# A transformer layer with experts on one core: the last tile's first norm, the routing plan and the end of the program

## The reference

```
x = x + xattn(layernorm(x), ctx, ctx)              # 16 heads, softmax, full context
x = x + linear_attn(layernorm(x))                  # elu features, cumulative k*v, its own layernorm
h = layernorm(x)
shared = (silu(h @ wg.T) * (h @ wu.T)) @ wd.T
topw, topi = top_k(sigmoid(h @ gate.T), 8);  topw /= topw.sum()
routed = sum over the 8: topw * ((silu(h @ eg[e].T) * (h @ eu[e].T)) @ ed[e].T)
x = x + shared + routed
```

## Time and profile before

| | us |
|---|---|
| median of 3 executions | 1316.6 (1314.49 to 1318.66) |
| the profiled execution | 1314.09 |
| its span, first to last instruction | 1312.2 |
| PE busy | 1231.6 (94%) |
| DVE busy | 743.8 (57%) |
| ACT busy | 593.5 (45%) |
| POOL busy | 395.9 (30%) |
| mean granted clock of PE, share of full | 0.986 |

### The profile page before, as it was taken

How to read it: one execution, slowest core, us unless ns; L and a number is a source line. 1 busy time by engine, 2 the same in 40 slices (tenths; PEclk the granted TensorE clock), 3 DMA queues, 4 the chain that set the end, 5 groups by cost and what they waited for, 6 DMA issues and landing times. The chain is left out here.

```text
span 1312.2 us, 32009 instructions
## 1 busy us (share of the span) xinstructions
PE 1231.6 (94%) x9830; PEld 926.3 (71%) x9831; DVE 743.8 (57%) x1645; ACT 593.5 (45%) x1184; POOL 395.9 (30%) x312
## 2 busy tenths in 40 slices
PE   5999999999999999999997789999999999999991
PEld 5888787877787878777875347766776676667660
DVE  4454765656657556565556656656555556556440
ACT  2443443433433434343341165667556666556540
POOL 0001021030020200300203224557554656556531
PEclk9999999999999999999999989999999999999996
DMA  6631200111102102101031177999999999999875
GB/s 224 279 125 35 68 20 17 68 35 35 52 18 68 34 3 68 36 26 52 2 106 33 57 251 246 314 317 344 301 302 285 310 330 335 337 270 323 260 189 88
DMA packets 67370, 205.44 MB, mean 157 GB/s; under 512 B 16064, under 2 KB 18496, under 8 KB 56913
## 3 DMA queue, kind: packets, MB, share of 16 engines
q1 hardware_dynamic: 43392, 159.78, 33.7%
q0 software_dynamic: 23888, 44.40, 16.2%
HBM read 177.32 MB, written 37.03 MB: 163 GB/s over the span
## 5 line engine op out<-in xcount | busy, mean ns | idle before, releaser
L452 POOL TENSOR_TENSOR rstd<-vep,half 128x1 f32<-128x1 f32 x32 | 20.7, 647 | 604.3 <-DVE vep L618 604.3
L917 PE MATMUL bank<-ch,wkh 128*128 128x256 f32 x512 | 157.1, 307 | 9.9 <-DVE cl L633 6.4
L543 ACT ACTIVATE kt<-bank,colb 128x256 f32<-128x256 f32 x128 | 60.5, 473 | 222.4 <-PE bank L919 222.4
L1621 PE MATMUL ebank<-guh,xth 128*128 128x512 f32 x380 | 155.5, 409 | 1.3 <-DVE xtl L1482 0.8
L1477 DVE TENSOR_TENSOR gul<-wgu,guh 128x2048 fp32r<-128x2048 f32 x54 | 123.8, 2292 | 53.7 <-ACT guh L1393 44.3
L1322 POOL DMA_INDIRECT xg<-xn_rows,ig x95 | 124.5, 1311 | 92.2 <-issue 60.6
L1623 PE MATMUL ebank<-guh,xtl 128*128 128x512 f32 x380 | 149.7, 394 | 0.0
L1622 PE MATMUL ebank<-gul,xth 128*128 128x512 f32 x380 | 148.9, 392 | 0.0
L918 PE MATMUL bank<-cl,wkh 128*128 128x256 f32 x512 | 144.9, 283 | 0.0
L919 PE MATMUL bank<-ch,wkl 128*128 128x256 f32 x512 | 144.9, 283 | 0.0
L1651 PE MATMUL ebank<-wd,ht 128*128 128x512 f32 x292 | 134.3, 593 | 0.8 <-ACT ht L1378 0.8
(11 more groups left out here) (242 smaller groups left out, 2475.4 us busy)
## 6 DMA issues: line engine op xcount, KB each, us to landing
wgu<-in_egu SPq DMA_DIRECT2D x54, 1024.0 KB
wd<-in_edn SPq DMA_DIRECT2D x54, 512.0 KB
sgu<-in_egu SPq DMA_DIRECT2D x17, 1024.0 KB
craw<-in_ctx SPq DMA_DIRECT2D x32, 514.0 KB, 3.3
sdn<-in_edn SPq DMA_DIRECT2D x17, 512.0 KB
wqkv<-in_wqkv SPq DMA_DIRECT2D x1, 3072.0 KB, 18.6
second_sums<-x1b SPq DMA_DIRECT2D x9, 256.0 KB, 4.0
xa<-in_x SPq DMA_DIRECT2D x8, 256.0 KB, 2.9
```

The lines of the kernel that those rows point to most:

```text
L917: mm(out, wkh[:, c, w], h[:, c, :], start=c == 0, stop=False)
L1621: mm(out, ah[:, c, :], bh[:, c, :], start=c == 0, stop=False)
```

## The change

Four edits:

1. The plan moves from the start of the second part into the first, as the function `plan()`, which DVE runs behind the shared addition of tile 2 (`PLAN` = 2) and so in front of that of tile 3. In the second part PE's four small products stand first.
2. Tile 7's first norm takes its statistics (`moments`) straight behind the addition; the waits for the store of `xn` and for `x3T` stand behind them, in front of the operation that writes `xn` (`normed`).
3. On POOL tile 7's residual moves ahead of tile 6's `outproj` roots, behind the last maximum of the attention (`s_nb`); its `xr` is loaded at tile 6's step `v`. Tile 7's `x1b` waits until `xn` has been written.
4. The second block is made with `no_gpsimd_drain=True`.

The split of the shared tiles, four and four, is the same in both kernels.

The diff. Of the plan's own lines, which are the same in both places, the first and the last stand:

```diff
@@ -79,6 +79,7 @@
 
 
 BIAS = 2
+PLAN = 2
 EARLY = K
 WRITE = 8
 
@@ -387,7 +388,7 @@
                     sp.dma_start(d.acc[bass.ds(t * P, P), :], x2[:, :]).then_inc(s_ys, 16)
                     if type(t) is int and t == NT - 2:
                         load_shared(t, d.sx[t - SHA], d.sy[t - SHA], d.s_sl)
-                if n == "outproj":
+                if n == ("v" if type(t) is int and t == NT - 2 else "outproj"):
 
                     xe_wait(sp, "oproj", t, tick)
                     if type(t) is not int or t + 1 < NT:
@@ -476,11 +477,15 @@
 
                     root(norm_pre(t))
 
+            def residual(t):
+                wait(pool, s_xr, 16 * (t + 1), tick)
+                nc.gpsimd.tensor_tensor(xr[:, :], xr[:, :], rowb[:, 0, :], ALU.add).then_inc(s_xb, 1)
+
             def on_post(n, t):
                 if n == "oproj":
                     wait(pool, s_wrest, 16 * 7)
-                    wait(pool, s_xr, 16 * (t + 1), tick)
-                    nc.gpsimd.tensor_tensor(xr[:, :], xr[:, :], rowb[:, 0, :], ALU.add).then_inc(s_xb, 1)
+                    if not (type(t) is int and t == NT - 1):
+                        residual(t)
                     root(norm_post(t, 0))
                     xe_wait(pool, "oproj", t, tick)
                     pool.wait_ge(s_blank, 16 * (NT + 1))
@@ -492,7 +497,12 @@
                                                          compute_op=ALU.add).then_inc(dumped, 16)
                         for dumped in d.s_dumped:
                             pool.wait_ge(dumped, 16)
+                    if type(t) is int and t == NT - 1:
+                        pool.wait_ge(s_xn, 2 * t + 1)
                     nc.gpsimd.tensor_tensor(x1b[:, :], x1[:, :], rowb[:, 4, :], ALU.add).then_inc(s_x1b, 1)
+                if n == "outproj" and type(t) is int and t == NT - 2:
+                    pool.wait_ge(s_nb, NB)
+                    residual(t + 1)
                 if n == "outproj":
                     root(norm_post(t, 1))
                     root(norm_post(t, 2))
@@ -620,6 +630,10 @@
             def norm(src, dst, count, ready):
 
                 moments(src)
+                normed(src, dst, count, ready)
+
+            def normed(src, dst, count, ready):
+
                 wait(dve, s_rstd, count + 1)
                 ins = V.tensor_scalar(dst[:, :], src[:, :], mv[:, 0:1], rstd[:, 0:1], ALU.subtract, ALU.mult)
                 if ready is not None:
@@ -743,10 +757,11 @@
                     wait(dve, s_x1b, t)
                     V.tensor_tensor(x1[:, :], out[:, :], xr[:, :], ALU.add).then_inc(done, 1)
 
+                    moments(x1)
                     wait(dve, s_xns, 16 * t, tick)
                     if final:
                         px_wait(dve, "x3T", t - 1)
-                    norm(x1, xn, norm_post(t, 0), s_xn)
+                    normed(x1, xn, norm_post(t, 0), s_xn)
                 if n in ("q", "k"):
                     j = "qk".index(n)
                     px_wait(dve, n, t)
@@ -846,6 +861,41 @@
                         px_wait(dve, "count", t)
                         V.tensor_copy(d.cnt[:, :], px[LAST_BANK["count"]][:, 0:E])
 
+            def plan():
+                dve.drain()
+                cnt, more, more2, end, start, own, picked, q4, col = d.cnt, d.more, d.more2, d.end, d.start, d.own, d.picked, d.q4, d.col
...
+                V.scalar_tensor_tensor(col[:, 1:2], rem, float(P), valid, ALU.is_gt, ALU.mult).then_inc(d.s_picked, 1)
+
             def on_shared(n, j, c):
                 k = j % 2
                 if n == "gu" and c == DC - 1:
@@ -857,6 +907,8 @@
                 if n == "down":
                     dve.wait_ge(s_sd, j + 1)
                     V.scalar_tensor_tensor(sy[j], sd_ps[:, :], 0.5, sy[j], ALU.mult, ALU.add).then_inc(s_sy, 1)
+                    if j == PLAN:
+                        plan()
 
 
             dve.wait_ge(s_pads, 16 * (NT + 1))
@@ -1192,7 +1244,7 @@
         s_slots = [sem(f"slots_in{i}") for i in range(2)]
         s_last = sem("last_slot_in")
         biased = [(s, BIAS) for t in tiles for n, s in t.s.items() if n != "y_ready"] + [(s, BIAS) for s in s_w.values()] + [(s_go, BIAS + NY)]
-        block = ctx.enter_context(nc.Block())
+        block = ctx.enter_context(nc.Block(no_gpsimd_drain=True))
         steps = NI // U + 1
         BOUNDED = "the plan bounds them"
 
@@ -1500,39 +1552,6 @@
                     ins = V.tensor_copy(ia[item.q][:, h:h + 1], c)
                 ins.then_inc(s_ia, 1)
 
...
-            V.scalar_tensor_tensor(col[:, 1:2], rem, float(P), valid, ALU.is_gt, ALU.mult).then_inc(d.s_picked, 1)
             V.memset(itab[:, :].rearrange("a (t n) -> a t n", n=4 * (P + 1))[:, :, 0:4], 0)
             V.memset(row[0:1, 0, 0:E], 1.0)
             V.tensor_scalar(row[0:1, 1, 0:E], cnt[0:1, :], float(P), None, ALU.is_gt)
@@ -1681,14 +1700,14 @@
                     last = mm(sd_ps[j % 2][:, :], tiles[j % 2].ht[:, c, :], sdn[:, c, :], start=c == 0, stop=c == IC - 1)
                 last.then_inc(s_sd, 1)
 
+            pe.wait_ge(d.s_picked, 1)
+            for f in range(4):
+                last = mm(bank[7][0:1, f * E:(f + 1) * E], col[:, f:f + 1], ident[:, 0:E], start=True, stop=True)
+            last.then_inc(s_turned, 1)
             pe.wait_ge(d.s_sl, 32 * SHB)
             for j in range(2):
                 shared_turn(j)
             shared_gu(0)
-            pe.wait_ge(d.s_picked, 1)
-            for f in range(4):
-                last = mm(bank[7][0:1, f * E:(f + 1) * E], col[:, f:f + 1], ident[:, 0:E], start=True, stop=True)
-            last.then_inc(s_turned, 1)
             for j in range(2, SHB):
                 shared_turn(j)
             for j in range(1, SHB):
```

More of the change, by code:

```diff
@@ L847, in on_post @@
                         V.tensor_copy(d.cnt[:, :], px[LAST_BANK["count"]][:, 0:E])
+            def plan():
+                dve.drain()
+                cnt, more, more2, end, start, own, picked, q4, col = d.cnt, d.more, d.more2, d.end, d.start, d.own, d.picked, d.q4, d.col
+                V.tensor_scalar(more[:, :], cnt[:, :], float(BLK), None, ALU.is_gt)
+                dve.drain()
+                a, spare = more, more2
+                for m in range(2, JB):
+                    V.scalar_tensor_tensor(spare[:, :], cnt[:, :], float(BLK * m), a[:, :], ALU.is_gt, ALU.add)
+                    dve.drain()
+                    a, spare = spare, a
+                V.tensor_tensor_scan(end[:, :], ones[:, 0:E], a[:, :], 0.0, ALU.mult, ALU.add)
+                dve.drain()
+                V.tensor_tensor(start[:, :], end[:, :], a[:, :], ALU.subtract)
+                dve.drain()
+                V.tensor_scalar(spare[:, :], start[:, :], pidx, None, ALU.is_le)
+                dve.drain()
+                V.scalar_tensor_tensor(own[:, :], end[:, :], pidx, spare[:, :], ALU.is_gt, ALU.mult)
+                dve.drain()
+                for f, values in enumerate((iota_e, start[:, :], cnt[:, :], ones[:, 0:E])):
+                    V.tensor_tensor(picked[:, f, :], values, own[:, :], ALU.mult)
+                dve.drain()
+                V.tensor_reduce(q4[:, :], picked[:, :, :], AX.X, ALU.add)
+                dve.drain()
+                e, first, held, valid = (q4[:, i:i + 1] for i in range(4))
+                block_nr, rem = col[:, 4:5], col[:, 5:6]
+                V.tensor_scalar(block_nr, pidx, 1.0, first, ALU.add, ALU.subtract)
+                V.tensor_copy(col[:, 0:1], valid)
+                V.tensor_copy(col[:, 2:3], e)
+                dve.drain()
+                V.scalar_tensor_tensor(rem, block_nr, float(-BLK), held, ALU.mult, ALU.add)
+                V.scalar_tensor_tensor(col[:, 3:4], block_nr, float(2 * E), e, ALU.mult, ALU.add)
+                dve.drain()
+                V.tensor_tensor(col[:, 3:4], col[:, 3:4], valid, ALU.mult)
+                V.scalar_tensor_tensor(col[:, 1:2], rem, float(P), valid, ALU.is_gt, ALU.mult).then_inc(d.s_picked, 1)
             def on_shared(n, j, c):
```

32 lines of the change are left out of this document (removed).

## The result

The changed kernel takes **1304.95 us** (median of 7 executions, 1303.02 to 1307.23), the kernel before 1314.38 in 7 executions (1310.74 to 1318.66, the three shown above among them). The ratio is **0.9941, 95% interval 0.9926 to 0.9956**: 7.8 us less, 5.8 to 9.7. The profiled execution took 1304.77 us with a span of 1302.8, so 1.97 us lie outside the span, against 1.89 before. Its span is 9.4 us shorter, more than the ratio says.

The account below looks back on a forecast made before the run. PE, busy 94% of the span, was taken to bound the kernel, except at the dip between its parts and the end. The sum, -2.45 + 2.7 + 0 - 7.06 = -6.8 us from 1316.6, gave 1309.8 us, range 1305 to 1314.5.

Parts of the forecast that it names:

- What bounds the kernel: Whole kernel: PE busy 94% of the span, so a microsecond counts only in the dip between the parts or at the end.
- The norm, 2.45 us: Tile 7's first norm, end of first part: last `xn` ends at 697.02 against 699.48, 2.45 us gained.
- the forecast's lower end: Last first-norm: smallest gain expected, 1.25 us from the wait for the `xn` store alone; the upper end was 2.7.
- The plan, 2.7 us later: Before the fourth shared addition: the moved plan delays it from 750.59 to 753.3, 2.7 us lost; 0 returns behind the seam.
- The seam at 756.65: Handover from first part to second: it hardly moves, 756.40 to 756.65, as the norm's gain pays for the plan.
- the forecast's 0.25 more: Norm and plan together: 2.45 us gained and 2.7 lost, the seam moving from 756.40 to 756.65.
- The clock, 0 between 1.4 lost and 3.1 won: PE behind the seam: longer idle could cost 1.4 us at half clock or win 3.1; 0 was taken.
- The drain, 7.06 us: POOL at the second block's exit: the DRAIN of 7.06 us goes, with 0 of it paid at program end.
- The first rival: Program end: the drain is owed anyway behind the last instruction, time 1316.9 us; chance 0.10.
- More is won in the middle, 1306.3 us: DVE's 4.57 us idle before L778 and 1.7 us of idle behind the seam: some 3.5 us less; chance 0.12.
- The slower side, 1319.1 us: Second part: three more 1.2 GHz spells in the expert rounds, 3.1 us each, take the gain; chance 0.04.
- The plan held by POOL's slot writes: Before the seam: the plan runs only behind POOL's slot transfers, seam 6.1 us later than forecast, 1315.9 us; chance 0.05.

## Why the prediction was right, and where it was wrong

- **What bounds the kernel**: right. PE stays busy behind the seam, and what the last exit loses is gained one for one.
- **The norm, 2.45 us**: the size holds (2.27 in the trace, without the 0.44 that were won ahead of it), both `xn` writes take 0.55 us, and the router beside `x1b` lost no more than 0.3 us (a CAST of 0.47 us). But the part of the statistics was mis-sized: the forecast's lower end gave "1.25 us (the wait alone)", and with POOL's edits in place the moved wait was worth 0 in that profile, where the store landed in 2.0 us. The forecast took 2.67 us for the landing from one profile; it is 2.0 to 4.0, and with it what the wait costs. By itself the moved wait is worth 0.6 us in a profile with a landing of 2.0 us, and more with a later one. In time the norm alone gave 4.3 us, with 2.45 outside the interval of 3.0 to 5.6. By the estimate above 2.6 of that are time saved as forecast, with the late landings in it, and 1.8 are clock, for which the forecast had no term. Why the clock gains is less clear. The lower clock followed at once in the two profiles in which PE had waited 4.72 us (the plan alone) and 2.11 us (the moved wait alone) for this `xn`, for some 3.4 us each, and in none in which it had waited about 1 us; but after 3.27 us and 2.74 us (the drain alone) it didn't follow either, so this is no more than a guess.
- **The plan, 2.7 us later**: right in the trace, 2.60. In time it cost 2.4 us on top of the norm's edits, and 0.65 and at most 2.5 without them; 0.2 us comes back behind the seam, and why the second is so small is open. Nobody waits for the tables: they come 7.4 us sooner, and the first expert product stands 28 to 31 us behind the seam in all kernels, the shortest where the clock stayed full.
- **The seam at 756.65**: 756.12. The norm pays for the plan. Together they give 1.4 us in time (from 0.5 more to 3.3 less), an interval that holds the forecast's 0.25 more.
- **The clock, 0 between 1.4 lost and 3.1 won**: 0.4 won. It had risen neither before PE resumed nor later than before. (By the earlier trace rows the spell before was 6.1 us of work and not 6.3.) That 0.4 is luck of one pair: in the 13 profiles with an idle spell of 5 us or more at the seam PE then worked for 2.9 to 6.1 us at the lower clock, a swing of 1.6 us between nearly equal kernels.
- **The drain, 7.06 us**: right; 6.9 in the span, 6.2 (3.9 to 8.5) in time alone. The first rival, the drain owed outside the span, falls: 1.7 to 2.1 us lie there in every execution, with a drain and without.
- **More is won in the middle, 1306.3 us**: the measured time is nearer to this number than to the forecast's, but by luck. What the rival named isn't there: PE still stood idle for 4.34 us in tile 7's linear attention, and for 0.75 and 0.93 us ahead of the expert transposes.
- **The slower side, 1319.1 us**: no more of the second part ran at the lower clock than before. The prediction counted this rival as slower, but it is 2.5 us above 1316.6, below the 3.95 us that it says can't be told from none, so its 0.04 belonged to "same".
- **The plan held by POOL's slot writes**: falls. The plan took 4.43 us beside the writes and 4.69 alone. The Trainium skill (SBUF — State Buffer, "SBUF: two separate sides") would have DVE's two-port operations hold up POOL's descriptors. POOL in the changed kernel, one write beside the plan and the last one behind it:

```profile
747.04 0.95 POOL L463 DMA_INDIRECT slot_table<-entry,idx  x1 [0.30 <-issue]
...
750.84 0.96 POOL L463 DMA_INDIRECT slot_table<-entry,idx  x1 [0.30 <-issue]
```

  0.95 beside 0.96 us: the writes aren't held either. Whether the plan's small operations are of the two-port kind no run shows. By the exclusive lock of the same section the two `xn` writes should shrink once POOL's additions are gone from beside them, and 1.48 to 0.55 us agrees.
- **The time itself**: the measured median is 4.9 us below the forecast. Most of that is the point it was counted from: the kernel before took 1316.6 in the three executions shown, and 1310.74 to 1314.38 in the four later ones, mean 1312.5. 6.8 less than that is 1305.7, and 1304.95 was measured. No term of the sum failed in size by more than 0.5 us in the trace; the 1.6 us in the rounds and the 0.44 ahead of the norm are no terms of it, and belong to no edit as far as is known. What failed was to take the median of three executions, which lie 4 us apart, as the fixed point, and to set the range's low end 4.8 us below it.

Open: why the last drain takes 7057 ns every time when all has landed; the idle time in the linear attention of tile 7 (4.57 us of DVE before, 4.34 us of PE after, for which the trace has no releaser), which stands in the profiles of the kernels before and after and in none of the experiments, so that it wasn't met there; and what decides whether the lower clock follows a wait of 1 to 3 us.

## What to carry to other kernels

Before work is moved ahead of a point where all engines meet, find which engine arrives there last and what stands in its chain; then cut the work to the gaps in front of it, as this list of dependent small operations could be cut. Where a wait and a slow neighbour stand in one place, remove the neighbour first and see whether there is a wait left, in several executions, since the landing of one transfer can take twice as long in one as in another. A term of 1 to 3 us read from one pair of profiles is no better than the clock and the landings in them. At a program's end a drain is worth looking for: it adds in full, if all that it could wait for has been waited for.

## What the runs showed of the hardware

- A drain on POOL behind the last landed transfer took 7.057 us, the same to the nanosecond in five kernels on four chips; the one at the seam ended 5.4 us behind the last slot write.
- In 13 profiles PE idled for 5.18 to 9.84 us at the seam and then ran at the lower clock for 2.9 to 6.1 us of work, without order between the two (5.3 behind 8.41 us, 6.1 behind 5.85, 2.9 behind 6.11); in the one in which it idled for 3.37 us it kept the full clock.
- Behind a wait of 1.06 to 1.94 us in the expert rounds PE's clock fell for some 3.4 us in 3 of 14 profiles, and in 11 it didn't.
- One POOL operation of 1.26 us beside a DVE write of 0.55 us made that 1.48; two such pairs, with the store and the wait behind the first, delayed PE by 1.8 us (7.01 against 5.20 us, the store landing in 2.0 us in both).
- The same store of `xn` (256 KB) landed 2.0 us behind its issue in 10 of 14 profiles, and 2.5 to 4.0 us behind it in the others, between runs of nearly the same code.
